# Extra unread bf16 matmuls on TensorE in the first layer's attention and ahead of its down products

## The reference, cut to what matters

```python
fused = bitnet_linear(text_embeddings, W_txt, b_txt)
for Wa, ba in ((W_att0, b_att0), (W_att1, b_att1)):
    kv = bitnet_linear(image_embeds, Wa, ba)
    k = jnp.concatenate([kv, kv], axis=-1)
    scores = jnp.einsum('bse,bpe->bsp', fused, k) * inv_sqrt_e
    attn = jax.nn.softmax(scores, axis=-1)
    fused = fused + 0.1 * jnp.einsum('bsp,bpe->bse', attn, k)
...
up = act_qdq(x @ lpbq_dequant(w_up).T)
gate = act_qdq(x @ lpbq_dequant(w_gate).T)
sig = fixed_qdq_u16(jax.nn.sigmoid(gate))
gate = act_qdq(gate * sig)
o = act_qdq(gate * up)
return o @ lpbq_dequant(w_down).T
```

## Time and profile before

| what | value |
| --- | --- |
| median of three runs | 1296.91 us |
| lowest and highest | 1296.06, 1301.83 us |
| the profiled execution | 1296.64 us |
| its span, first to last instruction | 1294.9 us |
| mean granted clock of TensorE | 0.802 |

### The profile page before, as it was taken

How to read it: one execution, slowest core, us unless ns; L and a number is a source line. 1 busy time by engine, 2 the same in 40 slices (tenths; PEclk the granted TensorE clock), 3 DMA queues, 4 the chain that set the end, 5 groups by cost and what they waited for, 6 DMA issues and landing times.

```text
span 1294.9 us, 22960 instructions
## 1 busy us (share of the span) xinstructions
PE 896.7 (69%) x7815; PEld 721.9 (56%) x7818; DVE 797.8 (62%) x1904; ACT 477.3 (37%) x1085; POOL 233.0 (18%) x280
## 2 busy tenths in 40 slices
PE   0336335048994783889975779993899999739992
PEld 0216122046763772556653679992677777628771
DVE  3864878966885235888776636555766566462334
ACT  0441308114552452344341343331343344205551
POOL 1000000000000671000000047760000000006771
PEclk9756668567995895677586789995999999659996
DMA  7200000006001118000000101118000000001113
GB/s 190 80 1 1 0 1 0 0 1 147 0 1 33 44 49 234 1 1 0 0 1 0 33 27 47 47 42 213 2 2 0 0 0 0 11 27 45 51 51 109
DMA packets 73143, 48.25 MB, mean 37 GB/s; under 512 B 19642, under 2 KB 65732, under 8 KB 73092
## 3 DMA queue, kind: packets, MB, share of 16 engines
q1 hardware_dynamic: 64484, 31.80, 9.2%
q0 software_dynamic: 6656, 13.64, 3.5%
q10 hardware_dynamic: 1952, 2.15, 0.5%
HBM read 33.93 MB, written 13.63 MB: 37 GB/s over the span
## 4 chain that ended last, share of the span: by engine, by line
PE 47%; DVE 27%; POOL 9%; issue 7%; ACT 6%; DMA 2%; DVEq 0%; SPq 0%; another core or an unknown queue 0%; POOLq 0%; ACTq 0%
PE ps L1909 6%; POOL rows_y L499 4%; POOL arena L494 4%; PE ps L1773 3%; PE ps L1742 3%; PE ps L1803 3%; PE ps L1923 3%; PE ps L1498 3%; PE ps L1762 3%; PE ps L1699 2%; PE ps L1709 2%; PE ps L1787 2%; PE ps L1726 2%; PE ps L1751 2%; DVE bst L523 2%
## 5 line engine op out<-in xcount | busy, mean ns | idle before, releaser
L1909 PE MATMUL ps<-arena 128*128 128x128 f32 x1152 | 153.8, 284 | 0.0
L494 POOL DMA_INDIRECT arena<-rows_x,row_in x104 | 102.8, 988 | 276.7 <-DVEq L1116 245.9
L1909 PEld LDWEIGHTS ps<-arena 128*128 128x128 f32 x1152 | 141.4, 197 | 1.4
L499 POOL DMA_INDIRECT rows_y<-arena,row_out x104 | 108.9, 1047 | 56.4 <-issue 21.3
L1923 PE MATMUL ps<-arena 128*128 x832 | 116.1, 283 | 1.4 <-DVE arena L1079 1.3
L1066 DVE COPY arena<-arena 128x644 f32 (+1 forms) x104 | 61.9, 595 | 78.1 <-DVE arena L1079 31.9
L1923 PEld LDWEIGHTS ps<-arena 128*128 128x128 f32 x832 | 102.1, 193 | 6.0 <-issue 3.3
L1498 PE MATMUL ps<-ident,xh 128*128 128x128 f32 x128 | 36.9, 446 | 85.9 <-DVE xh L555 69.8
L1314 ACT ACTIVATE arena<-arena 128x512 f32<-128x512 f32 (+1 forms) x96 | 53.7, 559 | 111.5 <-DVE arena L838 111.2
L1440 ACT ACTIVATE arena<-ps,arena 128x128 f32<-128x128 f32 x256 | 73.2, 368 | 46.9 <-PE ps L1909 46.9
L1773 PE MATMUL ps<-arena 128*64 128x64 f32 x768 | 71.3, 256 | 19.7 <-ACT arena L1318 16.2
(11 more groups left out here) (289 smaller groups left out, 1770.2 us busy)
## 6 DMA issues: line engine op xcount, KB each, us to landing
arena<-rows_y SPq DMA_DIRECT2D x20, 256.0 KB, 4.6
arena<-in_L_ffn_w SPq DMA_DIRECT2D x2, 2048.0 KB, 9.5
arena<-in_L_ffn_w SPq DMA_DIRECT2D x16, 256.0 KB, 6.5
rows_x<-xh SPq DMA_DIRECT2D x3, 1024.0 KB, 5.4
rows_x<-zero SPq DMA_DIRECT2D x1, 2560.0 KB, 9.9
arena<-in_L_ffn_gate_proj SPq DMA_DIRECT2D x8, 256.0 KB, 4.9
arena<-in_L_ffn_up_proj SPq DMA_DIRECT2D x8, 256.0 KB, 4.8
arena<-in_L_ffn_down_proj SPq DMA_DIRECT2D x1, 2048.0 KB, 9.9
```

The lines of the kernel that those rows point to most:

```text
L494: g.indirect_dma_start(xq[:, q % 4, :], None, rows_x, bass.IndirectOffsetOnAxis(row_in[:, q:q + 1], 0)).then_inc(sem(f"xq_loaded{q % 4}"), 16)
L499: g.indirect_dma_start(rows_y, bass.IndirectOffsetOnAxis(row_out[:, q:q + 1], 0), yq[:, q % 4, :], None).then_inc(sem(f"y_scattered{q % 4} ...
L1909: ins = pe.matmul(ps[:, 2 * m + s_ % 2, P * f:P * f + P], wst[:, s_ % 4, lo:lo + P], xqT[:, s_ % 2, :], start=True, stop=True)
```

## The change

The helper `dense` moves up, ahead of everything that TensorE does, so that the first layer can use it. Three uses are added. In each round of the first attention 16 of its matmuls stand behind the scores, ahead of the wait for the first half of the probabilities, and 4 stand ahead of the wait for the second half. Ahead of the down products TensorE waits for the third `scale_ready`, and then issues 10 matmuls before the first chunk's wait and 4 before each of the other two. The banks that they write (2 and 3, then 4 to 6) are not being read there.

```diff
+            def dense(bank, n):
+
+                for _ in range(n):
+                    pe.matmul(ps[:, bank, GT:2 * GT], onesb[:, :], q0[:, 0:GT], start=True, stop=True)
...
                     if g % 4 == 3:
                         ins.then_inc(sem("s0_mm"), 1)
+                dense(2, 16)
                 for u in range(2):
+                    if u:
+                        dense(3, 4)
                     pe.wait_ge(sem("s0_prob"), 2 * r + u + 1)
                     for g in range(4):
                         ins = pe.transpose(ps[:, 2 + u, P * g:P * g + P], prob[:, 512 * u + P * g:512 * u + P * g + P],
...
+            pe.wait_ge(sem("scale_ready"), 3)
             for f in range(NI):
+                dense(4 + f, 10 if f == 0 else 4)
                 pe.wait_ge(sem("o_ready"), f + 1)
                 for c in range(NC):
                     for k in range(4):
...
-                def dense(bank, n):
-
-                    for _ in range(n):
-                        pe.matmul(ps[:, bank, GT:2 * GT], onesb[:, :], q0[:, 0:GT], start=True, stop=True)
```

## The result

The changed kernel takes 1292.03 us in the median of 20 runs (1281.63 to 1300.52), the kernel before 1301.07 us in 20 runs of its own (1293.96 to 1309.24). The ratio is 0.9918, with a 95% interval from 0.9895 to 0.9941: the change makes the kernel 0.8% faster, about 10.7 us with an interval from 7.7 to 13.7 us, where 9.1 us (0.7%) had been forecast. The two medians lie 9.0 us apart. The two profiled executions differ by more, 12.4 us in their spans (1294.9 and 1282.5), and it is worth seeing where.

A forecast was written before the change was run, and what follows sets the result against it. No engine fills the span; the first attention is a strictly serial chain with products at the low clock. Gains of 7.9 us there and 1.2 us at the down products, 9.1 us from 1296.64, give 1287.5 us; 8-in-10 range 1283 to 1297.

The forecast's parts named there:

- The filler is hidden in the attention: First attention: the 16 take about 1.9 us, done 1.0 us before the first probabilities arrive; no cost on the path.
- It holds the clock, and the products take 3.77 us: First attention: clock stays at 1.00 through transposes and products, which take 3.77 instead of 7.08 us, 3.31 us per round.
- The 4: Ahead of the second transposes: 0.5 us, no cost; idle time there falls from 0.90 to 0.4 us, helping hold the clock.
- The second scores at the high clock, 0.4 us: First attention, second round: scores take about 1.9 instead of 3.56 us, softmax starts up to 0.8 us earlier; 0.4 taken.
- The down products, 1.2 us: Path to the first finished bank: 9.96 against 11.20 us, the clock rising 1.5 us in, with 0.96 us of filler.
- Later stages, 3 us either way: Work behind the change moves forward some 9 us and meets the clock at other points; 3 us allowed either way.
- one round only: Rival, first attention: the clock is lost in one round, so one 3.8 us gain and the 0.4 go; 1291.7 us, chance 0.17.
- The clock doesn't care: Rival: the clock falls behind the filler as before, only the down products change; about 1296.5 us, chance 0.10.
- The filler is paid and nothing comes back: Rival, slower side: at the low clock filler delays second transposes 1.6 us in all, plus down-product cost; 1299.6 us, chance 0.07.
- a case from the Trainium skill: Weighed rule: 2 us bursts with data waits between start cold, so the attention's products would stay at the low clock.

The follow-up runs named there:

- the kernel with the attention alone: Changed kernel without the wait and filler at the down products, against the kernel before on its chip: 1332.4 us against 1344.27, ratio 0.9926.
- the kernel with 32 rows: Filler in the first attention only, each matmul on 32 of 128 array rows, nothing at the down products: attention 35.8 us, products 7.09 us in both rounds.
- the changed kernel again: The unaltered changed kernel run once more on the third chip, against the kernel before there (1299.96 us): 1291.08 us, ratio 0.9927.

## Why the prediction was right

The time was inside the range and near the forecast, and the mechanism was the one named. Step by step:

- *The filler is hidden in the attention.* Right. The 16 took 1.92 us (1.9 forecast) and left 1.67 us of idle time ahead of the transposes; in the profile before, where the clock rose only at the end of the scores, it would have been about 1.0. The kernel with the attention alone is the closer picture of that: 2.25 us with a part at the low clock, and 0.88 us left.
- *It holds the clock, and the products take 3.77 us.* Right to the hundredth, 3.77 in both rounds; the factor of 0.53 from the nearest f32 row carried over to products of another shape. Eight executions with the 16 at full rows in both rounds (six kernels, two of them profiled twice) all had 3.8 us in both, so it wasn't a lucky one.
- *The 4.* Their cost was right (none), their role was not: I had let both groups share the work, and the 16 alone do it. With the 4 alone the clock was low every time when the products began, and rose in their first 1.1 us in three rounds of four.
- *The second scores at the high clock, 0.4 us.* Mostly wrong: the clock was lost between the rounds and was 0.57 over these scores. They took 3.2 to 3.6 us in all seven executions with the 16 in both rounds and no filler ahead of the scores, but 2.08 us in the kernel with filler in the first round only, whose first round is the same; why it was kept there is not shown. From the second scores to their second transposes it took 8.01 us instead of 8.17, 0.16 us. The same stretch of the first round was shorter by 0.89 us, because the clock was up at 96.49 already; that is the execution, not the change. Attention in all: 8.58 - 0.89 = 7.7 us, with 7.9 forecast. The other executions bear it out: those seven took 26.6 to 27.9 us for the attention, 27.2 in the mean, and the two executions without filler there 35.2 and 34.5 us, which is again 7.7 us.
- *The down products, 1.2 us.* This term of the sum was too large. The profile shows 0.73, and the kernel with this part alone 0.05% ± 0.27%. The rise did come earlier, 2.2 to 2.7 us behind the start of the products in the three executions with the filler as in the change, as forecast between 0 and 3.3; with the 10 alone it came at 3.5. But without filler there it came at 5.9 to 6.2 us in six executions and at 3.4 in two. Seven of these eight are further ones; they took 9.9 to 11.3 us beside the 11.2 of the profile before, two of them under 10: in some the products find the clock early without help, and then the 0.88 us of filler inside the path eats what it gives. The mean of the eight is 10.9 us, of the three with the filler (10.5, 10.3, 10.5) 10.4, a gain of 0.5 us. I had taken the gain against one execution, one of the six with the late rise, as if it were the mean, and the rise with filler nearer to the start of the products (1.5 us) than it came.
- *Later stages, 3 us either way.* Right in size for the median; two executions can differ by more. The largest part is the stretch with the third layer's attention. Over the same stretch, from the last scatter of the second layer to the first gather of the third, the changed kernel had in its first profile and in its second:

```profile
478.80:743.80 265.00, 194.07 (x1270) 141.17 (x1270) 192.89 (x483) 96.27 (x212) 6.97 (x10) 0.68 0.11 32
```

```profile
481.60:753.40 271.80, 202.68 (x1270) 146.14 (x1270) 193.54 (x483) 96.06 (x212) 6.99 (x10) 0.65 0.11 32
```

The same 1270 matmuls, nearly the same VectorE, and 6.8 us between them at a mean clock of 0.68 and 0.65. The kernel before took 265.6 us for it. The change has no instruction there. Differences of this size between executions of one kernel are enough to hide 2 us won elsewhere in a median of 12.

By its parts the gain comes to 7.7 us in the attention and 0.5 us at the down products, 8.2 us. The medians give 9.0 us, and the interval of the ratio holds both. That the forecast of 9.1 us met the medians to 0.1 us is luck: its down term was 0.7 us too large and its scores term 0.2 us, and the later stages, which no term covers, move the time by more than that.

The rivals: *one round only* was not seen in any execution with the 16 in both rounds, and the kernel with the filler in one round shows what it would have been, 29.6 us for the attention. *The clock doesn't care* fell with the first profile. *The filler is paid and nothing comes back* exists, in the kernel with 32 rows, and costs 1.3 us in the two rounds together, where 1.6 had been reckoned; with full rows its condition, a low clock over all of the 16, was met in no execution (they took 2.35 us at most), so its price there is not shown. The prediction also weighed a case from the Trainium skill ("TensorE: Matmul & The Clock Gate", section "HAM oscillation — how this bites in real kernels"), in which each wait of 3 to 5 us behind a burst of some 2 us makes the next burst start cold. The trace agrees with it in the second round of the kernel with filler in the first round only: behind a gap of 3.54 us the products ran at 0.50. The prediction stretched that case too far when it drew from it that products behind gaps of about 1 us would stay at the low clock: the gaps that the filler left (1.67 us ahead of the transposes, 1.9 us ahead of the down products) are shorter than the waits of that case, and the clock was kept over them. The 2.92 us at 209.63, which the prediction held against the case, are shorter than its waits too. Idle time is not all that counts either: in the kernel with 32 rows the clock was lost in a gap of 1.68 us.

## What to carry to other kernels

Where a serial chain alternates short matmul bursts with softmax on the other engines, look at the granted clock of each burst. Unread matmuls that use the whole array, put into the wait *ahead* of a burst, can nearly halve the burst (7.08 to 3.77 us here), and cost nothing as long as they end before its data arrive; between bursts that already follow without a gap they are pure cost (0.88 us here). Measure the gain of one wait against several executions, since one profile may have met the clock at its worst or best.

## What the runs showed of the hardware

- TensorE's busy time alone did not decide. With 32 of 128 rows the same matmuls for the same 1.92 us did not hold the clock (one execution, the first round; in the second it was low from the scores on), with 128 rows they did in every execution. The 64-row products ran 7.09 us without a gap at 0.50 in every round without filler in the attention and did not lift it.
- Chips differ, and not by TensorE's work. The kernel before took 1344.27 us on one chip and 1299.96 us on another. The windows over the three stages with gathers and scatters by row sum up to 339.6 us on the first (attention alone) and 295.4 us on the other (the changed kernel again):

```profile
sum 339.60, PE 271.79 PEld 254.19 DVE 111.01 ACT 129.66 POOL 210.37; mean PE 90.60 PEld 84.73 DVE 37.00 ACT 43.22 POOL 70.12
```

```profile
sum 295.40, PE 264.55 PEld 247.11 DVE 115.90 ACT 134.72 POOL 208.80; mean PE 88.18 PEld 82.37 DVE 38.63 ACT 44.91 POOL 69.60
```

That is 44.2 us, while the whole spans differ by 37.6, since the second execution was 6.6 us slower elsewhere. One kernel, the 16 alone, was profiled on the 1345.78 us chip and on the 1299.96 us chip: from the first gather to the last scatter of these stages it took 342.8 and 295.5 us, with spans of 1331.1 and 1288.8 us. So the extra time of the slower chips lies in these stages. GpSimd's busy time in the windows is nearly the same, 210.4 and 208.8 us; what is longer is the waiting. Why was not tried. It means that a time is worth something only beside a run of the kernel before on the same chip.
